# Causal attention with layer norms and a merged feed-forward: the row maximum first and in BF16, denominators in four column groups, sums two units later

## The reference

```python
h = layernorm(x)
q, k, v = split(h @ W_qkv)                 # 16 heads of 64
score = einsum('bihd,bjhd->bijh', q, k) / 8
w = softmax(causal(score), axis=2)         # over the keys j
x = x + (einsum('bijh,bjhd->bihd', w, v).reshape(b, l, 1024) @ W_out)
x = x + layernorm(x) @ W.T + b + layernorm(x) @ (up_aux @ lora_up @ lora_down @ down_aux).T
```

## Time and profile before

| | |
|---|---|
| median of 3 runs | 1910.45 us (1909.38 to 1913.12) |
| the profiled execution | 1910.15 us, its span 1908.1 us |
| busy share of the span | TensorE 96%, VectorE 67%, GpSimd 51%, ScalarE 42% |
| granted TensorE clock | 0.991 over the span |

### The profile page before, as it was taken

The page is one execution under the profiler, slowest core; times in us unless marked ns, Lnnn a source line. Parts: engine busy times, 40 slices in busy tenths (PEclk is TensorE's granted clock), DMA queues, the critical chain, the costliest instruction groups (busy, mean ns, idle before and its releaser), DMA issues. The chain is left out here.

```text
span 1908.1 us, 34290 instructions
## 1 busy us (share of the span) xinstructions
PE 1833.8 (96%) x13464; PEld 1128.0 (59%) x13464; DVE 1272.3 (67%) x2123; ACT 806.7 (42%) x982; POOL 972.8 (51%) x532
## 2 busy tenths in 40 slices
PE   7999998999999999999999999999999999998998
PEld 5877776555555555555555555555555555554897
DVE  5364652868676767676776767686777676747565
ACT  3222123454545454545454454545454545454221
POOL 1011000666675858575665666666758585746211
PEclk9999998999999999999999999999999999998999
DMA  5646445212121212222121312121212121023551
GB/s 204 223 179 232 164 157 210 68 35 78 41 73 46 72 46 68 62 58 67 46 74 51 80 45 79 40 74 46 67 46 73 46 68 51 24 73 102 177 192 56
DMA packets 150782, 171.33 MB, mean 90 GB/s; under 512 B 44618, under 2 KB 91744, under 8 KB 150624
## 3 DMA queue, kind: packets, MB, share of 16 engines
q1 hardware_dynamic: 150624, 169.15, 28.0%
HBM read 97.02 MB, written 71.57 MB: 88 GB/s over the span
## 5 line engine op out<-in xcount | busy, mean ns | idle before, releaser
L1017 DVE TENSOR_REDUCE f_part_max<-b_ring 128x1 f32<-128x512 f32 (+3 forms) x1200 | 675.3, 604 | 317.5 <-PE b_ring L850 213.5
L948 ACT ACTIVATE b_probs<-b_scores 128x1024 f32<-128x1024 f32 (+3 forms) x640 | 567.4, 898 | 615.5 <-PE b_scores L822 357.9
L1123 POOL TENSOR_TENSOR b_sum_pool<-b_sum_pool,b_probs 128x1024 f32<-128x1024 f32 x237 | 569.2, 2402 | 32.1 <-POOL b_sum_pool L1123 0.5
L1123 POOL TENSOR_TENSOR b_sum_pool<-b_probs 128x1024 f32<-128x1024 f32 x48 | 115.7, 2411 | 324.8 <-DVE g_sum_dve L1049 308.7
L822 PE MATMUL b_scores<-f_split 64*128 64x512 f32 (+2 forms) x1920 | 269.5, 383 | 9.1 <-ACT b_probs L948 7.3
L822 PE MATMUL b_scores<-b_split 64*128 64x512 f32 (+2 forms) x1920 | 268.0, 381 | 3.3 <-ACT b_probs L948 3.1
L886 PE MATMUL b_o_acc<-b_probs,f_v_in 128*64 128x512 f32 (+3 forms) x1280 | 270.5, 544 | 0.0
L886 PE MATMUL b_o_acc<-b_probs,b_v_in 128*64 128x512 f32 (+3 forms) x1280 | 269.0, 541 | 0.7 <-ACT b_probs L948 0.7
L1049 DVE TENSOR_TENSOR g_sum_dve<-g_sum_dve,b_probs 128x768 f32<-128x768 f32 (+3 forms) x243 | 229.5, 944 | 34.1 <-ACT b_probs L948 26.1
L822 PEld LDWEIGHTS b_scores<-b_split 64*128 64x128 f32 x1920 | 165.6, 185 | 51.0 <-issue 20.4
L822 PEld LDWEIGHTS b_scores<-f_split 64*128 64x128 f32 x1920 | 168.2, 187 | 46.0 <-issue 19.4
(11 more groups left out here) (135 smaller groups left out, 2288.5 us busy)
## 6 DMA issues: line engine op xcount, KB each, us to landing
f_raw<-k_t SPq DMA_DIRECT2D x32, 512.0 KB, 4.8
f_raw<-q_t SPq DMA_DIRECT2D x32, 512.0 KB, 5.6
g_recip<-r_t SPq DMA_DIRECT2D x128, 128.0 KB, 3.0
o_t<-g_o_norm SPq DMA_DIRECT2D x64, 256.0 KB, 2.0
q_t<-a_stage_a SPq DMA_DIRECT2D x32, 256.0 KB, 2.4
q_t<-a_stage_d SPq DMA_DIRECT2D x32, 256.0 KB, 2.0
k_t<-a_stage_a SPq DMA_DIRECT2D x32, 256.0 KB, 2.0
k_t<-a_stage_d SPq DMA_DIRECT2D x32, 256.0 KB, 2.0
```

The lines of the kernel that those rows point to most:

```text
L948: nc.scalar.activation(probs[s % PR][:, :, off:], scores[s % 2][:, :, off:], ACT.Exp, scale=scale).then_inc(exp_done, 1)
L1017: nc.vector.tensor_reduce(part_max[:, h, ib, c:c + 1], rowwise[h][:, 0:width], AX.X, ALU.max).then_inc(chunk_reduced, 1)
L1123: nc.gpsimd.tensor_tensor(sum_pool[:], first, probs[s % PR][:], ALU.add).then_inc(pool_added, 1)
```

## The change

Four things change in `attention`.

1. `shift` and the constant become BF16. The maximum is split into a high and a low BF16 row (`max_high`, `max_low`), so `place_max` has four DMAs and `take_rows` one more VectorE instruction. The maximum's pair of matmuls comes first in the score unit, with `start=True`, and a chunk that stood ahead of unit s+2 now stands between it and the other three terms.
2. `denominators` makes four products, 32 columns by 256 queries each, in place of two of 64 by 512. ScalarE's copy is half as wide, and four DMAs spread it in place of two.
3. VectorE takes the sum of unit s-2 in slot s (`SUM_LAG`), behind the reductions of that slot. Everything behind the denominators (their product, copy, inverse, `normalise`) moves by two units too.
4. The second diagonal pair of a tile has its small chunk one place later (`.sB` for `s.B`). `wo_hi` gets memory of its own.

```diff
-                want = "s.B" if t else "..B"
+                want = ".sB" if t else "..B"
...
                     for h in range(2):
-                        sp.dma_start(halves(shift[u][h * D:h * D + 1, :]).rearrange("o (b i) -> o b i", i=P),
-                                     halves(max_rows[h * KB:(h + 1) * KB, :])).then_inc(max_placed[u], 16)
+                        for i, rows in enumerate((max_high, max_low)):
+                            sp.dma_start(shift[u][h * D + i:h * D + i + 1, :].rearrange("o (b i) -> o b i", i=P),
+                                         rows[h * KB:(h + 1) * KB, :]).then_inc(max_placed[u], 16)
...
-                    for term, (a, b) in enumerate(((k_hi, q_hi), (k_hi, q_lo), (k_lo, q_hi), (None, shift))):
+                    for h in range(2):
+                        nc.tensor.matmul(scores[s % 2][:, h, lo:TILE], consts["first_rows"][head(h), :],
+                                         shift[u][head(h), queries], start=True, stop=False)
+                    for k in between:
+                        chunk(n + 1, 1 - u, k)
+                    for term, (a, b) in enumerate(((k_hi, q_hi), (k_hi, q_lo), (k_lo, q_hi))):
...
-                    for h in range(2):
-                        last = nc.tensor.matmul(denom[head(h), :], consts["ones"][:, 0:D],
-                                                sum_dve[t % 2][:, h, :], start=True, stop=True)
+                    for c in range(4):
+                        h, half = divmod(c, 2)
+                        cols = slice(half * DEN, (half + 1) * DEN)
+                        last = nc.tensor.matmul(denom[c * P // 4:(c + 1) * P // 4, 0:DEN], consts["ones"][:, 0:P // 4],
+                                                sum_dve[t % 2][:, h, cols], start=True, stop=True)
...
-                        for late in late_tile(n, s, previous):
+                        for late in late_tile(n, s - SUM_LAG, previous):
                             denominators(*late, n, ring_before[following]["denom", late[1]])
...
-                        if dve_adds(n, s):
-                            add_unit(n, s)
-                        for late in late_tile(n, s - 5, previous):
+                        for unit in units_summed_at(n, s):
+                            if dve_adds(*unit):
+                                add_unit(*unit)
+                        for late in late_tile(n, s - 5 - SUM_LAG, previous):
                             reciprocals(*late)
```

More of the change, by code:

```diff
@@ L31 @@
 STAGES = 3
+DEN = TILE // 2
 LOADS = 2
@@ L818, in score_unit @@
                     diagonal = j >= NB * t
-                    for term, (a, b) in enumerate(((k_hi, q_hi), (k_hi, q_lo), (k_lo, q_hi), (None, shift))):
+                    for h in range(2):
[4 more added lines that the diff above has]
+                    for term, (a, b) in enumerate(((k_hi, q_hi), (k_hi, q_lo), (k_lo, q_hi))):
                         for h in range(2):
-                            lhs = consts["first_row"][head(h), :] if a is None else a[u][head(h), keys]
-                            last = nc.tensor.matmul(scores[s % 2][:, h, lo:TILE], lhs, b[u][head(h), queries],
-                                                    start=(term == 0), stop=(term == 3 and not diagonal))
+                            last = nc.tensor.matmul(scores[s % 2][:, h, lo:TILE], a[u][head(h), keys],
+                                                    b[u][head(h), queries], start=False,
+                                                    stop=(term == 2 and not diagonal))
                     if diagonal:
@@ L903, in item @@
                         places = plan[s // 2] if following else ((), (), ())
+                        assert s + AHEAD < U or not any(places)
                         for e in range(2):
-                            for k in places[e]:
-                                chunk(n + 1, 1 - u, k)
                             ahead = s + e + AHEAD
                             if ahead < U:
-                                score_unit(n, u, ahead)
+                                for k in places[1] if e else ():
+                                    chunk(n + 1, 1 - u, k)
+                                score_unit(n, u, ahead, () if e else places[0])
                             elif following:
@@ L1338, in _ @@
                 pe.wait_ge(tail["dve_added"], tail["dve_ops"])
-                for h in range(2):
-                    half = slice(h * P // 2, (h + 1) * P // 2)
-                    last = nc.tensor.matmul(last_denom[half, :], consts["ones"][:, 0:P // 2],
-                                            tail["sum_dve"][last_t % 2][:, h, :], start=True, stop=True)
+                for c in range(4):
+                    h, half = divmod(c, 2)
+                    cols = slice(half * DEN, (half + 1) * DEN)
+                    last = nc.tensor.matmul(last_denom[c * P // 4:(c + 1) * P // 4, :], consts["ones"][:, 0:P // 4],
+                                            tail["sum_dve"][last_t % 2][:, h, cols], start=True, stop=True)
                 last.then_inc(tail["denom_made"], 1)
```

88 lines of the change are left out of this document (53 added, 35 removed).

## The result

| | before | after |
|---|---|---|
| median | 1910.48 us (1909.38 to 1913.12, 4 runs) | 2029.45 us (2024.81 to 2036.3, 4 runs) |
| span of the profiled execution | 1908.1 us | 2034.2 us |
| granted TensorE clock over the span | 0.991 | 0.965 |

The ratio is 1.0623 (95% interval 1.0591 to 1.0656): the changed kernel is slower by 119 us. The forecast was 1973, +63, with a range to 2016. An item takes 98.0 us (items 1 to 14, mean) and took 89.9; 15 times 8.1 is 121, so all of the loss is made anew in each item of `attention`.

What follows compares the result with a forecast made beforehand. TensorE, busy 97.8% in mid-`attention`, was taken as the bound, so waits put on it cost in full. Terms -21 - 10 + 20 + 41 + 33 = +63 on 1910 gave 1973 us, range 1915 to 2016.

Steps and rivals of the forecast that it cites:

- The sum.: Whole kernel: -21 denominators, -10 maximum's term, +20 chunk behind it, +41 later sums, +33 late maxima: +63 us.
- The sums two slots later: Three sums between reductions of pairs 22 and 24: +1.1 twice an item (pairs 12, 24), +33; pair 4, +8.
- If `reciprocals` in slot 11 comes before their landing VectorE waits below 1, 15 times, within the bound: VectorE's possible wait for the denominators' four spreading DMAs: below 1, 15 times, left without a price.
- What is late next: the maxima: Pair 38: GpSimd starts later, maxima DMAs land late, TensorE waits; 2.2 an item, 15 items, +33.
- the last rival: Everything costs more: port, wait for spread denominators, granted clock falling behind a long stall; 2016; chance 0.13.
- Denominators: Four half-wide products at once save 0.33 in each of 64 rounds: -21 us.
- The maximum's term: BF16 weights load faster: 0.05 at heads of 12 of 20 pairs, 16 items, -10; stream itself taken as 0.
- The chunk behind it: First chunk after the maximum's term in `BBB` and `BsB` pairs: 0.16 later, 8 times, 15 items, +20.
- The maxima come in time: Rival: GpSimd's start moves by less than 0.7 against TensorE, so no last stall; 1940; chance 0.15.
- VectorE takes the sums in its idle time: Rival: later sums cost nothing in pairs 4, 12, 24, and 0.75 returns in 10 and 22; 1909; chance 0.12.
- the BF16 term streams faster: Rival: each of 640 score units gains up to 0.11, -70; 1903 with the other terms; chance 0.07.
- Everything costs more: Rival: port, spread denominators' wait and falling clock; +60 and +50 for the large terms; 2016; chance 0.13.

Runs made afterwards that it cites:

- e3_er_fill: Changed kernel with maxima placed ahead of tile 2's store, reciprocals two slots later, and the maximum's matmuls made 8 times more in units 15 and 27: 1962.56 us.
- e2_den_max: Kernel before with 32-column denominators and the BF16 maximum first, chunk behind it; sums and small chunk in their old places: 1893.2 us.
- e1_lag_only: Kernel before with only the later sums (SUM_LAG = 2) and all that hangs on them: 2004.39 us.
- e2_fill: Changed kernel with the maximum's matmuls made 12 times more in units 15 and 27 and 24 times more in unit 39: 2048.29 us.
- e2_early: Changed kernel with the DMAs that place the maxima issued ahead of tile 2's store in SyncE's queue: 2000.53 us.
- e3_dm_chunk: e2_den_max with the first chunk of a pair again ahead of the whole score unit, the maximum's term still first in the unit: 1881.95 us.
- e1_den_only: Kernel before with only the 32-column denominators (four products, four spreading DMAs): 1895.61 us.
- e3_early_recip: Changed kernel with maxima placed ahead of tile 2's store and reciprocals two slots later: 1988.64 us.

## Why the prediction was wrong

The sign and the places of the two large stalls were right, and the size was half of the truth: the failed step is the term for the later sums, in which a wait for a DMA in VectorE's queue and the fall of the clock had no price. Step by step:

- **The sum.** -21 - 10 + 20 for the two small parts is -11; they measured -17. +41 +33 for what the later sums bring is 74; the whole change less those two parts (the small chunk's place is in it, which costs nothing beside the later sums) is 2029.45 - 1893.2 = 136. That is where it failed.
- **"The sums two slots later", +1.9 less 0.75 in pairs 12 and 24.** The place and the order were right, the term was mis-sized. Ahead of pair 24 the stretch takes 5.54 at the median where I had 5.35. I had named what lengthens it in eight of 14 items, a sum beside `normalise`, and left it out of the sum ("up to 0.7 each, some 10 us more"); it is 0.33 an item there, 5 us. Ahead of pair 12 the stretch takes 6.27, and there it is the wait of the next point. In `e3_er_fill`, with full clock and the maxima out of the way, the kernel is still 69 us above `e2_den_max` by the medians, and one sum of the three moved behind the reductions took 16 of them. In that kernel a sum meets `normalise` ahead of pair 12 in 13 of 14 items and ahead of pair 24 in 8, for some 0.9 each time, which is about 20 us (an estimate), and VectorE waits 1.1 for the spread denominators in pair 14. So what the later sums bring at full clock was about 69 and not 41; what of it is owed to the added matmuls themselves stays open.
- **"If `reciprocals` in slot 11 comes before their landing VectorE waits below 1, 15 times, within the bound".** It waited 0.71 to 1.83 (median 1.20), just ahead of what TensorE waits for. And slot 19, the same instruction for the next tile, I had not looked at: 1.98 at the median, and row 18 is 0.93 longer than before, some 14 us. I had the four DMAs' issue time as off the path; in `e1_lag_only`, with two DMAs, the wait is 0 at the median in pair 12 and 2.11 in pair 20, so it is the first that comes with the four DMAs. With the maxima out of the way this was 12 us; in `e2_fill` the wait in pair 20 grew, to 3.86 in item 5.
- **"What is late next: the maxima", 2.2 in pair 38.** Right in every link: GpSimd's first addition came 2.33 behind the chunk's load (2.3 forecast), and the load waited for the fourth DMA behind the store. The term +33 measured 29 in `e2_early`, while row 36 shows 3.7 an item, 56 us: at its own place the term was too small too, and row 24 took 18 us of it back. The trace has `normalise` at 1.73 for 1.29.
- **No price for the clock.** It stood in the last rival alone ("a stall long enough that the granted clock falls behind it", with 0.13). 26 us were measured for the two stalls that were left when the third was gone. A sum that ends with three stalls of 2 to 3 us in each item should have had it in the likeliest case.
- **Denominators.** From the last load of the products with v to the first load behind the round it was 1.82 (831.52 to 833.34) and is 1.52 (819.29 to 820.81 in `e3_dm_chunk`): 0.30 for a round, 0.33 forecast. (The 0.86 of the expectation is the two rounds' own time; from the first load it was 1.39 before, since that load came ahead of its turn.) 64 rounds are 19 us; 15 arrived in `e1_den_only`. Rows 8 and 20, in which VectorE sets the pace, took 0.2 each back.
- **The maximum's term.** Forecast +10, measured -4.5 alone. The chunk behind it cost 11 (20 forecast), so the term itself gained some 16 (10 forecast): four rows without such a chunk (2, 10, 34, 36) fell by 0.2 where I had 0.05 a head. The chunk cost 0.12 a row and not 0.16, and in pair 34 too, which I had left out; rows 8, 18 and 20 gave some of it back. Why the term's new place gains 0.2 was not tried.
- **Small chunk.** I gave its new place no term of its own. Beside the later sums that was right (-2 and inside the noise); with the sums in their old place it is 38.
- **Rivals.** "The maxima come in time" and "VectorE takes the sums in its idle time" are refuted by the rows above, "the BF16 term streams faster" at its price of 70 by -4.5. "Everything costs more" was the right one, and 13 us too low.

From after to before the steps are these, in us: early maxima -29, later reciprocals -12, work in the stalls -26, one sum behind the reductions -16. Then `e2_den_max`, which has no later sums and with them none of these four steps, and the small chunk in its old place: -54, which is 1893.2; then the chunk ahead, -11, which is 1881.95.

## What to carry to other kernels

Where several engines stand in each other's queues, a wait that is made longer can be paid three times, as here: by what stands behind it, by TensorE's clock after it, and by the next queue whose spare time it uses up. So price a stall's clock in the likeliest case, look at each instruction that waits for a DMA ahead of others in an in-order queue, and judge two repairs only together. Count over all items before the timeline of one is taken for the rule: item 5 shows a sum beside `normalise` that six of 14 items do not have. And time the parts of a change alone: here two of four gained, the small chunk's place cost 38 with the sums where they were and nothing beside the later ones, and the sum of the three single results was 45 us from the whole (-15 - 4.5 + 94 = 74 against 119).

## What the hardware showed that I had not expected

- 32 matmuls more in an item, placed in two stalls, made the kernel 26 us faster, with the granted clock at 1.00 in place of 0.97 from 500 to 1600 us (`e3_er_fill` against `e3_early_recip`).
- The size of what VectorE and GpSimd take from each other. The sum of 768 elements that starts at 874.15 beside `normalise` (873.97 to 875.26) ends at 876.08, that is 0.82 behind the product's end, and needs 0.95 by itself. In `e3_er_fill` the product starts at 814.41 within a sum that ends at 815.48 and ends 1.13 behind that; the next sum starts at 815.57 and ends 0.55 behind the product. Each seems to stand until the other is done, with some 0.1 saved. The Trainium skill (SBUF — State Buffer, SBUF: two separate sides) says that the one that comes second waits for the whole of the first; the trace agrees. I had that rule and left its price out of the sum.
- Four DMAs issued one behind the other, those that spread the denominators, took SyncE 2.39 (`e3_early_recip`), 3.17 (`e2_fill`) or 3.37 us (the changed kernel) for the same four.
